# A 32-row state product issued as four products, each on its own column group of TensorE

## The reference, cut to what matters

```python
def reference(x, ...):                       # x: 8 images of 32x32 positions, 128 channels
    x = _L0_conv_ref(x, ...)                 # attention inside each image
    t = _to_tokens(x)                        # 8 sequences of 1024 tokens
    t = t + _L1_attn_ref(_ln_t(t), ...)      # state-space layer, below
    t = t + _L1_ffn_ref(_ln_t(t), ...)       # 8 experts, the best 2 for each token
    return _from_tokens(t, x)

def _L1_attn_ref(...):                       # 8 heads of 32 values, 32 states for each value
    def step(state, inp):
        dA_t, dt_t, B_t, C_t, x_t = inp
        state = state * dA_t[:, :, None, None] + (dt_t[:, :, None] * x_t)[..., None] * B_t[:, None, None, :]
        y = jnp.einsum('bhpn,bn->bhp', state, C_t)
        return (state, y)
```

## Time and profile before

| | us |
|---|---|
| median of three runs | 1159.17 |
| lowest and highest run | 1157.26, 1159.95 |
| profiled execution, span from first to last instruction | 1156.2 |
| TensorE busy in the span | 1052.0 |
| VectorE busy | 840.3 |
| ScalarE busy | 760.0 |
| GpSimd busy | 625.2 |

### The profile page before, as it was taken

How to read it: one execution, slowest core, us unless ns; L and a number is a source line. 1 busy time by engine, 2 the same in 40 slices (tenths; PEclk the granted TensorE clock), 3 DMA queues, 4 the chain that set the end, 5 groups by cost and what they waited for, 6 DMA issues and landing times.

```text
span 1156.2 us, 28221 instructions
## 1 busy us (share of the span) xinstructions
PE 1052.0 (91%) x7924; PEld 957.2 (83%) x7924; DVE 840.3 (73%) x3054; ACT 760.0 (66%) x1914; POOL 625.2 (54%) x987
## 2 busy tenths in 40 slices
PE   4889999999999999999999999888889999999993
PEld 3678888888887888888888787777788999999893
DVE  3588888988988888898898888877535554444564
ACT  2677677777767867777776776666556666666551
POOL 8123443467557466656655745654755466444442
PEclk9999999999999999999999999989989999999997
DMA  7300000001000100100100000010112222223566
GB/s 216 72 3 29 12 3 30 7 25 41 10 30 10 41 20 12 48 7 26 40 15 25 9 23 11 16 45 28 42 52 64 65 80 80 78 73 101 169 183 186
DMA packets 66405, 58.66 MB, mean 51 GB/s; under 512 B 12869, under 2 KB 56429, under 8 KB 66253
## 3 DMA queue, kind: packets, MB, share of 16 engines
q1 hardware_dynamic: 48237, 34.54, 10.8%
q0 software_dynamic: 8704, 17.97, 4.7%
q10 hardware_dynamic: 9312, 4.33, 1.4%
HBM read 32.67 MB, written 25.21 MB: 50 GB/s over the span
## 4 chain that ended last, share of the span: by engine, by line
PE 47%; issue 17%; DVE 14%; POOL 12%; ACT 4%; DMA 3%; SPq 2%; DVEq 1%; POOLq 0%; ACTq 0%
PE pY L690 6%; PE pX L685 6%; PE pc L519 5%; PE pa L574 3%; PE pb L702 3%; PE pd L702 3%; DVE CV L1449 2%; PE pY L483 2%; DMA GX<-rows_by_expert 2%; POOL rows_by_expert L1165 2%; POOL YG L1103 2%; POOL st L1146 2%; PE pc L523 1%; POOL STE L1094 1%; PE pX L496 1%
## 5 line engine op out<-in xcount | busy, mean ns | idle before, releaser
L1054 POOL DMA_INDIRECT results_by_choice<-YE,DIX x144 | 144.5, 1003 | 147.3 <-ACT YE L948 120.4
L1165 POOL DMA_INDIRECT rows_by_expert<-XA,SL x128 | 148.1, 1157 | 36.8 <-issue 36.2
L1711 DVE TENSOR_TENSOR V<-XT,pY 128x384 f32<-128x384 f32 x132 | 73.1, 554 | 125.6 <-ACT XT L938 117.8
L519 PEld LDWEIGHTS pc<-XDT,M 128*128 128x128 f32 x1024 | 124.1, 193 | 12.9 <-issue 8.9
L1449 DVE SCALAR_TENSOR_TENSOR CV<-XBC,cw,CV 128x256 f32<-128x256 f32 x288 | 129.9, 505 | 0.0
L574 PE MATMUL pa<-V,PT 128*128 128x128 f32 x1024 | 128.9, 280 | 0.7 <-DVE XDT L1498 0.6
L519 PE MATMUL pc<-XDT,M 128*128 128x64 f32 x1024 | 122.9, 273 | 5.3 <-DVE CT L1455 5.3
L574 PEld LDWEIGHTS pa<-V,PT 128*128 128x128 f32 x1024 | 120.7, 193 | 3.4 <-issue 1.3
L1103 POOL TENSOR_TENSOR YG<-Y,SZ 128x256 f32<-128x256 f32 x64 | 46.4, 725 | 142.5 <-DVE Y L1485 128.8
L1460 DVE TENSOR_REDUCE NM<-pX 128x1 f32<-128x1024 f32 x64 | 78.1, 1220 | 48.7 <-PE pX L498 48.6
L930 ACT ACTIVATE XT<-pa 128x128 f32<-128x128 f32 x132 | 36.5, 277 | 106.4 <-PE pa L676 106.3
(11 more groups left out here) (322 smaller groups left out, 3043.3 us busy)
## 6 DMA issues: line engine op xcount, KB each, us to landing
GX<-rows_by_expert SPq DMA_DIRECT2D x144, 65.0 KB
XT<-in_xT_dram SPq DMA_DIRECT2D x8, 512.0 KB, 4.0
X<-in_x_dram SPq DMA_DIRECT2D x16, 256.0 KB, 3.0
out_dram<-T ACTq DMA_DIRECT2D x16, 256.0 KB
results_by_choice<-YE,DIX POOLq DMA_INDIRECT x144
rows_by_expert<-XA,SL POOLq DMA_INDIRECT x128, 2.6
XBC<-results_by_choice SPq DMA_DIRECT2D x8, 256.0 KB, 3.9
XA<-results_by_choice SPq DMA_DIRECT2D x8, 256.0 KB, 5.0
```

Source lines behind the costliest of these rows:

```text
L519: mm(pc[:, 64 * h:64 * h + 64], M[:, h, :], XDT[:, e % 2, HD * h:HD * h + 64], start=h == 0, stop=False, skip_group_check=True)
L1054: g.indirect_dma_start(yg, bass.IndirectOffsetOnAxis(ap=DIX[:, slot, :], axis=0), YE[:, slot, :], None).then_inc(s(f"ye{slot}_scattered"), 16)
L1165: g.indirect_dma_start(xg, bass.IndirectOffsetOnAxis(ap=SL[:, j // NT, j % NT:j % NT + 1], axis=0), XA[:, j // NT, j % NT, :], None).then_ ...
L1711: tt(HT[par].rearrange("p k t -> p (k t)"), SH[:, par, :], pY[:, 512 * par:512 * par + HP3], ALU.mult).then_inc(s("hh_ready"), 1)
```

## The change

The product of L646 is written as four. Product `j` takes the first 32 columns of `BNAT` as its stationary operand and the columns `64 j` to `64 j + 63` of `XW` as its moving operand; its result goes to the partitions `32 j` to `32 j + 31` of `pd`, always in the columns 256 to 319. The range of partitions of the output is the column group of TensorE that the product uses. The sum in L1653, and the copy in L1656, become four instructions of 32 partitions by 64 columns, each of which reads another range of partitions of `pd` and writes its 64 columns of `ST`, which lies as before. Semaphores, waits and their places stay as they are: `state_ps` rises with the last product, `st_ready` with the last sum.

```diff
@@ -15,6 +15,7 @@
     TAPS = 4
+    QUARTER = DI * NS // P
@@ -643,7 +644,8 @@
                     if k % NT != 0:
                         mm(pd[:, 0:DI], CTP[:, par, tk], ST[:], start=True, stop=True)
-                    last = mm(pd[:, DI:2 * DI], BNAT[:], XW[:], start=k % NT == 0, stop=True, skip_group_check=True)
+                    for j in range(DI // QUARTER):
+                        last = mm(pd[NS * j:NS * j + NS, DI:DI + QUARTER], BNAT[:, 0:NS], XW[:, QUARTER * j:QUARTER * j + QUARTER], start=k % NT == 0, stop=True, skip_group_check=True)
                     last.then_inc(s("state_ps"), 1)
@@ -1650,10 +1652,15 @@
                         upto(dve, "ste_ready", base, k + 1)
-                        tt(ST[0:NS, :], STE[0:NS, :], pd[0:NS, DI:2 * DI], ALU.add).then_inc(s("st_ready"), 1)
+                        for j in range(DI // QUARTER):
+                            cols = slice(QUARTER * j, QUARTER * j + QUARTER)
+                            last = tt(ST[0:NS, cols], pd[NS * j:NS * j + NS, DI:DI + QUARTER], STE[0:NS, cols], ALU.add)
+                        last.then_inc(s("st_ready"), 1)
                     else:
                         upto(dve, "state_ps", base, k + 1)
-                        v.tensor_copy(ST[0:NS, :], pd[0:NS, DI:2 * DI]).then_inc(s("st_ready"), 1)
+                        for j in range(DI // QUARTER):
+                            last = v.tensor_copy(ST[0:NS, QUARTER * j:QUARTER * j + QUARTER], pd[NS * j:NS * j + NS, DI:DI + QUARTER])
+                        last.then_inc(s("st_ready"), 1)
                         v.nop().then_inc(s("yo_ready"), 1)
```

## The result

The changed kernel takes 1178.8 us (median of four runs, 1178.14 to 1181.01), the kernel before 1158.22 beside it: 1.0174 times as long, 95% interval 1.0149 to 1.0198, some 20 us. The forecast was 1173.0, range 1161 to 1180. The time lies in the range, near its upper end, and the sign is right; the profile shows that the reason is not.

What follows compares the result with a forecast made beforehand. TensorE was taken to bound 46 of 64 tile steps, VectorE 18. Span 1156.2 + 11.0 (TensorE) + 3.6 (VectorE) = 1170.8, plus 3.0 around it, less 0.8 for near ties: 1173.0 us, range 1161 to 1180.

Steps and rivals of the forecast that it cites:

- 11.0 us for TensorE: TensorE's narrow products in place of L646: +0.24 us a tile in the 46 steps where TensorE counts.
- 3.6 us for VectorE: Four state sums instead of one at L1653: +0.20 us a tile in the 18 steps that VectorE bounds.
- The count of 18 and 46: Of 64 tiles, 18 steps where VectorE's part of the change counts, 46 where TensorE's does, read from the waits.
- TensorE, the switch: Changing to narrow columns and back around L646's products: 0.09 + 0.03 + 0.09 + 0.11 = 0.32 us a tile.
- The exposed load: First full weight load behind the narrow matmuls, no longer hidden under a matmul: 0.11 us a tile.
- TensorE, the eight matmuls: The narrow matmuls replacing L646: 0.22 to 0.43 us, middle way 0.27, against 0.43 removed.
- rival 4: Changing over costs half and groups overlap: TensorE -0.05 to +0.05 a tile, 1159 to 1163 us; chance 0.11.
- rival 1: Groups overlap down to the pace of L592: TensorE +0.11 a tile, 1167.7 us; chance 0.14.
- VectorE, the four sums: Four sums replacing L1653's 0.31 us take 0.50 to 0.56 us; +0.20 us a tile taken.
- What costs nothing: GpSimd gets `ST` 0.2 us later without cost; DMA queues and ScalarE unmoved; 384 more load and matmul pairs.
- The clock: Named danger: TensorE's clock might fall to its lower level because less of the array works; no size given.
- The signs named beforehand: Trace timings at TensorE's narrow loads and matmuls, VectorE's sums and TensorE-bound steps (11.4 us, about 0.24 longer) that would show the forecast.

Runs made afterwards that it cites:

- sums on one range: Kernel before with its one state sum split into four 32x64 sums that all read and write partitions 0 to 31; ratio 1.0052.
- VectorE's part alone: Kernel before with TensorE unchanged, but the state summed by four instructions reading partition ranges 0, 32, 64 and 96 (state wrong); ratio 1.0189.
- one column group: Against the kernel before: one product of 32 stationary by 256 moving columns on one column group, one state sum as before; ratio 1.0102.

## Why the prediction was right, and where it wasn't

The time held by luck, by two errors that in part made up for each other: the forecast's 11.0 us for TensorE measured between nothing and 3, its 3.6 us for VectorE about 20. The sum came out 6 us low, with nearly all of it in the wrong place.

**What bounds the kernel.** The reading held: a step pays for TensorE where VectorE waits for the scores, else for VectorE. The count of 18 and 46 held only for small changes. Of the 41 waits for the scores, 1.2 us on average, 14 were of only 0.2 to 0.4 us; VectorE's 0.60 us turned them into lateness, and by the same count 38 steps were bound by it. The three sizes of VectorE's part show it: +0.20, +0.46 and +0.60 us a tile cost 6, 10 and 22 us in the time (with intervals of 2 to 5 us on each side), and 3.5, 10.5 and 18.3 us in the sum of the 63 distances, that is 17, 23 and 30 us for each us. A fixed number of steps times a price is an account for small changes only.

**TensorE, the switch.** 0.09 in and 0.09 out, read from L606 and L663, measured 0.09 and 0.09 (the last of the eight starts 0.10 after the first load and streams 0.05; the next full load comes at 0.25). The exposed load was given 0.11, from L627; for L484 it is 0.06 (0.249 to 0.308, where its stream of matmuls, 0.109 apart, effectively begins), in even steps, before the decay sums, 0.11. The rows of a strange bf16 product and a strange one-column product were good witnesses.

**TensorE, the eight matmuls.** Here a step failed, the overlap: I took 0.27 to 0.43 us and called 0.22 the lower bound, by the pace of L592. The eight take 0.155: two sets of four, starts 0.007 us apart in a set, 0.08 from the first of one set to the first of the other. In odd steps TensorE has 0.09 + 0.155 + 0.09 + 0.06 = 0.40 us where the full product took 0.43, in even steps 0.45. L592's pace is that of full-width loads and bounds nothing for narrow ones on different groups. The Trainium skill's page TensorEngine Tiling (Array Packing), Key Properties, has both halves, the drain at a change of mode and the parallel tiles, and this case agrees with both; I priced only the first by rows. The balance, -0.03 to +0.015, has the size of rival 4, to which the prediction gave 0.11, but the cause of rival 1: the groups overlap, further than rival 1 had it, and changing over costs 0.24 to 0.29 us of the 0.32 forecast, not half.

**VectorE, the four sums.** The term was mis-sized threefold: 0.20 forecast, 0.60 measured. The 0.50 us for four short sums was right, and sums on one range have it. What was missing are four holds of about 0.1 us, one at each change of the range of partitions read from PSUM. None of the rows that I read changes its range, so none showed it, and I didn't bound it from above for that reason, although the change is made of four ranges. The rule stood in the Trainium skill, in the section on VectorE cited above, which I hadn't weighed.

**What costs nothing.** GpSimd's L1096 waits for the state 51.8 us in 17 times instead of 43.6, and L1105 for VectorE's output 141.2 instead of 128.8, as VectorE is later; no new line shows, and neither delays TensorE more than before.

**The clock.** The granted clock, which I had named as a danger, is a little lower on average in the profile after (0.973 against 0.982), by slices between 737 and 826 us. What it costs there can be read from one step of the expert phase, from 815.0 to 831.7 us, in which TensorE was at 1.2 GHz, the lower of its two levels, for 10.6 us; it had fallen to it at 811.9, at the end of a wait of 1.36 us. The step took 16.7 us, where before it took 12.0 with 0.7 us at that level (the 16 matmuls of L520 alone took 3.52 us instead of 1.90). Behind the last score product the kernel after loses 2.6 us up to this step and 4.6 in it and gets back 2.7 behind it: these are the 4.5 us that the 63 distances leave open. The other three runs of the kernel after had higher means (0.978 to 0.983) and spans of 1176.4 to 1177.0 us, 2 to 3 below the profiled one. So the clock makes some 2 to 5 us of the profiled difference, of which it isn't shown how much is due to the change: with VectorE's part alone that step takes 12.5 us, with one column group 16.8.

**The signs named beforehand.** Starts of 0.03 to 0.053 between the matmuls, 0.39 to 0.55 from the first narrow to the next full load, 11.4 us steps longer by 0.24: all three fail, though the total doesn't, and so does the fourth, 0.44 to 0.56 us for VectorE's sums (0.91). The two signs of the switch came true: the first narrow load at 0.308 where 0.31 was named, the next full load 0.148 after the last narrow start where 0.15 was. Only by such signs could the forecast be told from luck.

## What to carry to other kernels

Splitting a product over column groups of TensorE leaves its result on several ranges of partitions, and each VectorE instruction that picks them up from another range than the last one on PSUM read waits for that one to end (0.08 to 0.13 us here): price the reader, not only the product. A narrow product among full ones pays a switch on both sides, in all 0.27 to 0.31 us here as the kernel with one group has it; four groups on a product of 0.43 us only break even. And where two engines take turns at bounding a kernel, a second term in the wrong place can hide behind a right total: compare step by step.

## What the runs showed of the hardware

- Four column groups of TensorE work at the same time on fp32 operands: eight narrow matmuls (two passes of four) in 0.155 us, a second set for 0.11 more.
- Going from 128 stationary columns to 32, and back, costs 0.09 us each way, plus 0.06 to 0.11 for the first full load, in every one of the kernels with a narrow product.
- VectorE: short sums on PSUM with the same range start 0.11 to 0.13 us apart for 32x64; each change of the range read adds 0.08 to 0.13. All of them write partitions 0 to 31: it was not tried whether a change of the range written costs the same.
- TensorE's clock at 1.2 GHz for 10.6 us of a step lengthened it from 12.0 to 16.7 us.
